# Routing phase of an audio tower on one core: gate and up as products of split values, and ranks taken before statistics

## The reference

```
flat = layernorm(h).reshape(-1, 256)
gs = einsum('td,ndm->tnm', flat, wg_s)          # 2 shared experts, 128 wide each
us = einsum('td,ndm->tnm', flat, wu_s)
out = einsum('tnm,nmd->td', silu(gs) * us, wd_s)
probs = softmax(flat @ router_w)                # 16 routed experts, the best 2 per token
weights, indices = top_k(probs, 2); weights /= weights.sum() + 1e-9
out += routed experts of each token, weighted   # silu(flat@wg_r) * (flat@wu_r) @ wd_r
```

## Time and profile before

| what | value |
|---|---|
| median of 3 runs | 2036.21 us (2031.98 to 2040.96) |
| the profiled execution's own time | 2024.68 us |
| its span in the profile | 2023.0 us |
| mean granted TensorE clock | 0.951 of full speed |
| TensorE matmul busy | 1818.7 us (90%) |
| TensorE weight load busy | 1344.1 us (66%) |
| VectorE busy | 1380.3 us (68%) |
| ScalarE busy | 979.6 us (48%) |
| GpSimd busy | 958.0 us (47%) |

### The profile page before, as it was taken

One profiled execution on the slowest core, in us unless ns is written; L12 is line 12 of the kernel. 1 busy time (PEld: TensorE's weight loads), 2 busy tenths in 40 slices (PEclk: granted clock), 3 DMA queues, 4 the chain that ended last, 5 costly groups with the idle time before them and its releaser, 6 DMA issues. The chain is left out here.

```text
span 2023.0 us, 48610 instructions
## 1 busy us (share of the span) xinstructions
PE 1818.7 (90%) x14417; PEld 1344.1 (66%) x14418; DVE 1380.3 (68%) x3805; ACT 979.6 (48%) x2062; POOL 958.0 (47%) x1315
## 2 busy tenths in 40 slices
PE   4799999999999999999999999669999995988883
PEld 4667777777777777776777776345655663977773
DVE  3577887887887887887887786256766763355554
ACT  1165565565565565565565565322322320544441
POOL 4044444444444444444444445235666663266666
PEclk7799999999999999999999999669999997999997
DMA  2433343343343333333333332222332335799996
GB/s 77 85 135 121 124 141 119 124 140 119 125 139 119 127 137 120 128 136 120 129 134 120 121 131 98 65 94 95 112 104 100 110 107 154 234 319 328 325 319 221
DMA packets 214514, 291.08 MB, mean 144 GB/s; under 512 B 44854, under 2 KB 176666, under 8 KB 214426
## 3 DMA queue, kind: packets, MB, share of 16 engines
q1 hardware_dynamic: 178010, 186.11, 29.9%
q0 software_dynamic: 18048, 49.31, 7.6%
q10 hardware_dynamic: 18368, 54.64, 7.1%
HBM read 83.25 MB, written 129.69 MB: 105 GB/s over the span
## 5 line engine op out<-in xcount | busy, mean ns | idle before, releaser
L825 DVE TENSOR_REDUCE neg_max<-bank 120x1 f32<-120x376 f32 (+2 forms) x896 | 520.3, 594 | 214.5 <-PE bank L585 212.9
L734 ACT ACTIVATE probs<-bank 128x376 f32<-128x376 f32 (+2 forms) x896 | 450.2, 521 | 286.2 <-PE bank L619 275.2
L585 PE MATMUL bank<-k_rows,q_rows 64*128 64x128 f32 (+2 forms) x1536 | 405.3, 339 | 13.8 <-ACT probs L734 9.6
L619 PE MATMUL bank<-q_rows,k_rows 64*120 64x120 f32 (+2 forms) x1536 | 394.5, 344 | 2.9 <-ACT probs L734 2.5
L938 POOL TENSOR_SCALAR_AFFINE_SELECT probs<-probs 128x512 f32<-128x512 f32 (+1 forms) x384 | 233.3, 627 | 277.3 <-ACT probs L734 277.3
L602 PE MATMUL bank<-causal,own_row 64*120 64x120 bf16 (+4 forms) x1792 | 289.5, 242 | 15.0 <-DMA k_rows<-k_flat_hi 11.5
L585 PEld LDWEIGHTS bank<-k_rows,q_rows 64*128 64x128 f32 (+1 forms) x1536 | 238.1, 187 | 26.6 <-ACT probs L734 21.1
L1768 POOL DMA_INDIRECT x_sorted<-r_normed,route x188 | 183.3, 975 | 125.5 <-DVE route L1619 73.2
L602 PEld LDWEIGHTS bank<-causal,own_row 64*128 64x128 bf16 (+2 forms) x1792 | 151.4, 115 | 136.5 <-issue 68.9
L2124 POOL DMA_INDIRECT y_got<-y_sorted,p_route x188 | 182.7, 972 | 123.6 <-issue 121.7
L619 PEld LDWEIGHTS bank<-q_rows,k_rows 64*128 64x128 f32 (+1 forms) x1536 | 231.3, 185 | 9.0 <-ACT probs L734 5.4
(11 more groups left out here) (204 smaller groups left out, 3777.4 us busy)
## 6 DMA issues: line engine op xcount, KB each, us to landing
x_sorted<-zeros ACTq DMA_DIRECT2D x32, 816.0 KB, 3.9
y_sorted<-zeros ACTq DMA_DIRECT2D x32, 816.0 KB, 4.9
x_rows<-x_sorted SPq DMA_DIRECT2D x51, 512.0 KB
y_sorted<-p_y_rows SPq DMA_DIRECT2D x51, 512.0 KB
q_rows<-q_flat_hi SPq DMA_DIRECT2D x256, 94.0 KB
k_rows<-k_flat_hi SPq DMA_DIRECT2D x248, 94.0 KB
q_rows<-q_flat_lo SPq DMA_DIRECT2D x128, 94.0 KB
out_dram<-base SPq DMA_DIRECT2D x47, 256.0 KB
```

The lines of the kernel that those rows point to most:

```text
L585: last = eng.matmul(ps[0:T[t], m * w:(m + 1) * w], q[rows, slot, t * P:t * P + T[t]], k[rows, slot, 0:w], start=False, stop=(m == len(head ...
L619: last = eng.matmul(ps[0:T[t], m * w:(m + 1) * w], k[64 * c:64 * c + 64, slot, t * P:t * P + T[t]], q[64 * c:64 * c + 64, slot, t * P:S], ...
L734: eng.activation(probs[g % 2][0:T[t], first:first + len(heads), OFF[t]:OFF[t] + w], bank_exp[n % 2][0:T[t], 0:len(heads) * w].rearrange("k ...
L825: eng.tensor_reduce(dst, src, AX.X, ALU.max, negate=True).then_inc(max_taken, 1)
```

## The change

Gate and up of the shared experts are computed from split values. The weights are split once, at the opening: ScalarE copies each of the two weight tiles to an `F32R` tile (the high part), and VectorE subtracts it from the whole one (the low part). For every group `keep_T` makes two copies of each transposed half: the `F32R` high part in `nT_of`, and the whole float32 value in `nT`, which only `router` still reads and which is a single buffer now. A new VectorE operation, `keep_low`, subtracts the high part from the bank and writes the low part; it stands at the end of the step, after `hidden_of(1)`. `gate` and `up` become six matmuls each (two halves of three terms). `gated_of` writes over `tanh`, so `tanh_of` now waits for `hidden_done`. `normed_T` waits for `nT_lo` too, since `keep_low` reads the bank. On VectorE `take_ranks` comes ahead of `stats_of`. In the steps that call `clear`, `keep_low` stands ahead of it.

```diff
-        nT = [sb(f"r_normedT{p}", [P, 2, TILES * P]) for p in range(2)]
+        nT = sb("r_normedT", [P, 2, TILES * P])
+        nT_of = [[sb(f"r_normedT{p}_{part}", [P, 2, TILES * P], F32R) for part in ("hi", "lo")] for p in range(2)]
+        w_gate = [sb(f"r_gate_{part}", [P, 2, NS, P], F32R) for part in ("hi", "lo")]
+        w_up = [sb(f"r_up_{part}", [P, 2, NS, P], F32R) for part in ("hi", "lo")]
-        gated = [sb(f"r_gated{c}", [P, TILES * P]) for c in range(2)]
+        gated = tanh
 ...
+                def split_product(out, w, c, st, shift):
+                    n = tiles(st, shift) * P
+                    rows = nT_of[(st.b + shift) % 2]
+                    terms = [(i, j, k) for k in range(2) for i, j in ((0, 0), (0, 1), (1, 0))]
+                    for m, (i, j, k) in enumerate(terms):
+                        last = eng.matmul(out[:, 0:n], w[i][:, k, c, :], rows[j][:, k, 0:n],
+                                          start=(m == 0), stop=(m == len(terms) - 1))
+                    return last
                 def gate(st, c, shift=0):
+                    if c == 0:
+                        eng.wait_ge(nT_lo, st.at(shift, 2, 2))
-                    for k in range(2):
-                        last = eng.matmul(bank_gate[c][:, 0:n], experts.gate[:, k, c, :], src[:, k, 0:n],
-                                          start=(k == 0), stop=(k == 1))
-                    last.then_inc(gate_done, 1)
+                    split_product(bank_gate[c], w_gate, c, st, shift).then_inc(gate_done, 1)
                 def normed_T(st):
 ...
                             eng.wait_ge(nT_done, st.at(2, 2, j - 1))
+                            eng.wait_ge(nT_lo, st.at(2, 2, j - 1))
 ...
             def _(eng):            # ScalarE
+                eng.wait_ge(experts.loaded, experts.LOADS)
+                for parts, whole in ((w_gate, experts.gate), (w_up, experts.up)):
+                    eng.activation(parts[0][:, :, :, :], whole[:, :, :, :], ACT.Copy).then_inc(w_hi, 1)
 ...
                     if not st.before(0, 1):
-                        eng.wait_ge(gated_done, st.at(0, 2, c - 1))
+                        eng.wait_ge(hidden_done, st.at(0, 2, c - 1))
 ...
-                    eng.activation(nT[st.b % 2][:, j, 0:n], bank_T[j][:, 0:n], ACT.Copy).then_inc(nT_done, 1)
+                    eng.activation(nT_of[st.b % 2][0][:, j, 0:n], bank_T[j][:, 0:n], ACT.Copy)
+                    eng.activation(nT[:, j, 0:n], bank_T[j][:, 0:n], ACT.Copy).then_inc(nT_done, 1)
 ...
             def _(eng):            # VectorE
+                for n, (parts, whole) in enumerate(((w_gate, experts.gate), (w_up, experts.up))):
+                    eng.wait_ge(w_hi, n + 1)
+                    eng.tensor_tensor(parts[1][:, :, :, :], whole[:, :, :, :], parts[0][:, :, :, :].bitcast(F32),
+                                      ALU.subtract).then_inc(w_lo, 1)
+                def keep_low(st, j):
+                    n = tiles(st, 2) * P
+                    hi, lo = nT_of[st.b % 2]
+                    eng.wait_ge(nT_done, st.at(2, 2, j + 1))
+                    eng.tensor_tensor(lo[:, j, 0:n], bank_T[j][:, 0:n], hi[:, j, 0:n].bitcast(F32), ALU.subtract)\
+                        .then_inc(nT_lo, 1)
 ...
+                    if group:
+                        take_ranks(st)
                     if ahead:
                         stats_of(st)
                     if group:
-                        take_ranks(st)
                         sum_all(st)
 ...
                         hidden_of(st, 1)
+                    if st.runs(2, GROUPS):
+                        keep_low(st, 0)
+                        keep_low(st, 1)
```

More of the change, by code:

```diff
@@ L1249, in routing_phase @@
         nT_done = sem("nT_done")
+        nT_lo = sem("nT_lo")
+        w_hi = sem("r_w_hi")
+        w_lo = sem("r_w_lo")
         logits_done = sem("logits_done")
@@ L1289, in _ @@
                 eng.wait_ge(experts.loaded, experts.LOADS)
+                eng.wait_ge(w_lo, 2)
                 def router(st):
-                    src = nT[(st.b + 1) % 2]
+                    src = nT
                     eng.wait_ge(nT_done, st.at(1, 2, 2))
@@ L1301, in router @@
                     last.then_inc(logits_done, 1)
+                def split_product(out, w, c, st, shift):
[6 more added lines that the diff above has]
+                    return last
                 def gate(st, c, shift=0):
-                    src = nT[(st.b + shift) % 2]
-                    n = tiles(st, shift) * P
+                    if c == 0:
+                        eng.wait_ge(nT_lo, st.at(shift, 2, 2))
                     if not st.before(shift, 1):
                         eng.wait_ge(hidden_done, st.at(shift, 2, c - 1))
-                    for k in range(2):
-                        last = eng.matmul(bank_gate[c][:, 0:n], experts.gate[:, k, c, :], src[:, k, 0:n],
-                                          start=(k == 0), stop=(k == 1))
-                    last.then_inc(gate_done, 1)
+                    split_product(bank_gate[c], w_gate, c, st, shift).then_inc(gate_done, 1)
                 def up(st, c, shift=0):
-                    src = nT[(st.b + shift) % 2]
-                    n = tiles(st, shift) * P
                     if not (st.before(shift, 1) and c == 0):
                         eng.wait_ge(hidden_done, st.at(shift, 2, c))
-                    for k in range(2):
-                        last = eng.matmul(bank_up[:, 0:n], experts.up[:, k, c, :], src[:, k, 0:n],
-                                          start=(k == 0), stop=(k == 1))
-                    last.then_inc(up_done, 1)
+                    split_product(bank_up, w_up, c, st, shift).then_inc(up_done, 1)
                 def normed_T(st):
```

## The result

The changed kernel takes 2006.05 us (median of 4 runs, 2000.99 to 2016.2), the kernel before 2034.26 (4 runs, 2031.98 to 2040.96). The ratio is 0.9889, 95% interval 0.9842 to 0.9936: faster, by 13 to 32 us (the two medians lie 28.2 us apart, and the ratio puts the gain at 22.6). A second set of runs, with other runs of the kernel before, gave 2012.14 and a ratio of 0.9891 (0.9856 to 0.9925). So the direction was right and the size too small: 2023.5 was forecast, and the time lies under the whole range, 2014 to 2032. The profiled execution took 2003.71 us with a span of 2002.0, 21.0 under that of before, where 12.7 were worked out.

What follows compares the result with a forecast made beforehand. The prediction took the loop gate(0), tanh, VectorE, down to set each routing step, TensorE close behind. Plain steps 7.2, slow ones 2.8, early gates 1.7 and opening 1.0 sum to 12.7 us: 2023.5 from 2036.21, range 2014 to 2032.

Steps and rivals of the forecast that it cites:

- The loop gate(0), tanh, VectorE, down: Routing step: this chain sets the period, so only gate(0)'s saving counts, 0.40 us a step, to 13.5 us.
- the wait before D: TensorE's wait before down(0) starts a step: takes up 1.2 us saved in other products, growing from 0.24 to 1.4 us.
- The products: Gate and up on TensorE: six instructions at 0.22 us make 1.32 us against 1.72, 0.40 less a product.
- keep_low and keep_T in a plain step: VectorE's 1.2 us of subtractions and ScalarE's two more copies stay hidden; router does not wait.
- Where the loop turns: Three turns, VectorE's pause before router: keep_low's 1.2 us ahead against 1.3 us of statistics no longer behind; zero.
- the sum: Steps 2 to 22 and opening: 7.2 plain, 2.8 slow steps, 1.7 early gates, 1.0 opening; 12.7 us gained.
- Low clock: two turns at 1.4: Slow steps after some turns: up's excess falls into the wait before D; two steps gain 1.4 us instead of 0.40.
- The first steps: Half-clock gates in steps 1 and 2 gain 1.7 us, the opening 1.0; keep_low replacing statistics beside the clears, zero.
- all is gained: Rival: TensorE bounds the routing phase, four products save 1.6 us a step; 1999 us, chance 0.05.
- The hand-over through VectorE: Rival: keep_low waits for ScalarE or the turn's pause grows; from 1.1 us late the gain is gone, 2034; chance 0.07.
- The falling clock: Rival: the longer wait before D brings low clock in each step, costing 35 us; 2058 us, chance 0.08.
- The base: Whole kernel: the profiled execution lies 11.5 us under the median of runs, 2036.21, carried over to predict 2023.5.

Runs made afterwards that it cites:

- e3: Two kernels: the changed kernel with two more matmuls in gate(0) alone, 2020.56 us, or in each of up(0), gate(1) and up(1), 2039.26 us.
- e2: The changed kernel with stats_of put back ahead of take_ranks, so split products without the new order; 2035.15 us, ratio 1.0016.
- f6: The changed kernel with two unused VectorE sums, 1.2 us, added beside keep_low at the end of each step; 2024.76 us, ratio 0.9985.
- e1: The kernel before with take_ranks moved ahead of stats_of and nothing else; 2019.36 us, ratio 0.9934.
- e3 gate0: The changed kernel with two more matmuls in gate(0) alone; 2020.56 us, ratio 0.9957.
- e4: The changed kernel with both halves of VectorE's result moved right behind hidden_of(0); 2014.95 us, ratio 0.9903.
- e3_others_longer: The changed kernel with two more matmuls in each of up(0), gate(1) and up(1), not in gate(0); 2039.26 us, ratio 1.0044.
- e6: The same kernel as f6, run on another chip; 2184.77 us, ratio 1.0042.

## Why the size was wrong

Point by point, in the prediction's order.

*The loop gate(0), tanh, VectorE, down:* right. The two e3 kernels show it: work in gate(0) costs its full time, work in the other three goes into the wait before D. The plain step came out at 13.49 (forecast 13.5).

*The products:* six take 1.38 us, 0.23 each, where 0.22 was taken and 0.236 was the bound; gate(0) to up(0) fell from 1.79 to 1.47 us, 0.32 instead of 0.40. The step gained 0.43 all the same. `gated_of(0)` starts 2.30 us behind gate(0)'s start, for 2.62 before, which is that 0.32; and from there to D it is 5.48 us for 5.60, with `hidden_of(0)` 0.98 behind `gated_of(0)` for 1.09. Two small misses that cancel.

*keep_low and keep_T in a plain step:* right. `keep_low` waits for nothing, the ranks are 1 us early, and e2 measured 0.50 us for not moving them.

***Where the loop turns: zero.* This is the step that failed.** The prediction set `keep_low`, 1.2 us, against the statistics, 1.3 us, as if both stood in the same path. They don't. `keep_low` stands ahead of the branch and is done inside the pause (f6: 2.4 us are hidden there, and the pause takes 3.5 to 3.8 us for 3.3 to 3.6), while the statistics stood behind it, in front of the ranks for which `router` waits. So a turn gains about the whole 1.3 us: `router`'s waits at the three turns are 1.16, 1.45 and 1.40 us shorter, 4.0 us for the zero of the sum. The first turn shows it clean, both times at a clock of 1.00: 16.20 - 14.53 = 1.67 us, of which 1.84 - 0.68 = 1.16 are the shorter wait and 0.32 the shorter gate.

*Low clock: two turns at 1.4.* Missed for the same reason: I took the low-clock spells as given and let the split products shorten them. With the shorter wait they mostly did not come: the second and third turn gained 3.66 and 3.92 us. In all the turns gave 9.25 us for 3.2 forecast, and that is 6.05 of the 8.3 us missing in the sum: 4.0 of the 9.25 are the shorter waits, 1.0 the shorter gates, and most of the rest is the clock. Another 2.8 lie behind D22, in the spread of a stretch that the edits hardly touch. That the order works through the turns is shown by e1 and e2; that the shorter wait is what kept the clock up is likely, not shown: of 15 turns with a wait of 0.3 to 0.9 us (changed twice, e1, e3 gate0, f6) seven kept a clock of 1.00, of e4's three with 1.1 us one did, and of 21 with 1.6 us or more one did.

*The first steps:* 0.6 us for 1.7. The early gates are shorter, but the wait of `router` behind the clears grew by 0.7 us in all, 7.6 less the turns' 1.76 against 10.9 less 5.77. That `keep_low` in the place of the statistics costs nothing there was true only as a sum: e1 shows 7.5 us for the order alone, and the changed kernel, with `keep_low` put back in the same place, had lost them again.

*The rivals.* TensorE's busy share fell and only half of what it lost was time, so "all is gained" did not happen; that the total came near its 1999 us is the turns' doing, and that of the spread below. The hand-over through VectorE was not late in a plain step; its price was also mis-added: 1.1 us late is 0.4 over the slack, 8 us in 20 steps, which leaves 4.7 of the 12.7 us and 2031.5, not 2034. The falling clock did not come: the plain steps wait 1.15 and 1.51 us ahead of D and run at a clock of 1.00 (the window at 1455.90). By that, the rule of the Trainium skill (TensorE: Matmul & The Clock Gate, "A second HAM failure mode: psum-queue depth-cycling"), that frequent short idles between groups of matmuls let the clock swing, does not hold for one wait of such length in each step of this loop. In e2, with 0.23 us of wait before `router` added in each step, the clock did fall in three of 17 plain steps; what tells these three from the other steps is open.

*The base:* half of the distance in the median is no error about the kernel. The prediction carried the 11.5 us between the profiled execution of the kernel before and its median over to the changed kernel; there the median, 2006.05, lies 2.3 us over the profiled 2003.71. That is 9.2 of the 17.5 us between 2023.5 and 2006.05, and the sum's 8.3 are the rest. The executions spread by 9 us in the kernel before and by 15 in the changed one, so this part is luck, against the forecast this time. The 21.0 us between the two profiled executions lie outside the forecast 6 to 16 all the same.

## What to carry to other kernels

At a loop's turn ask of each instruction of the pausing engine on which side of the branch it stands: queued ahead of it, behind the last one that waits for its predecessor, it can be free; behind it and in front of what another engine waits for, it costs its full time, and low clock may follow. An exchange of equal work across such a point is no zero. And when an engine gets shorter work in return for more work on another, look for room in that other's order first: here the products alone brought nothing, the order alone 13 us, both 22.

## What the hardware showed that I had not expected

- VectorE's pause at a turn was 3.1 to 3.8 us in all 36 turns of the twelve traces other than e3_others_longer that have no late ScalarE, counted from the start of its last instruction that had to wait for its predecessor, whatever was queued behind it (0 to 2.4 us). In e3_others_longer it was 5.84, 5.75 and 5.56 us, in e6 4.52, 5.81 and 5.84.
- In each of these 42 turns one packet of the instruction queue q14 lies in the pause. In the 36 it comes 1.0 to 1.7 us behind the pause's start, and VectorE goes on 1.9 to 2.3 us after it; in e3_others_longer and in the last two turns of e6 it comes at 3.5 to 3.9 us, behind a burst of data transfers, and VectorE goes on 1.9 to 2.0 us after it. Only the first turn of e6, with 2.8 us after the packet, stands outside.
- After a turn the clock's spell costs more than the wait: 20.2 us a turn in e3_others_longer, 14.3 in the changed kernel at 1.00. Yet e1's first turn had low clock after a wait of only 0.62 us and f6's three after 0.62 to 0.90, so the wait alone does not decide it.
- On one chip ScalarE saw a TensorE result 4 to 7 us late in most steps, and the same kernels took 7% longer.
